# A convolution mixed by a softmax over kernel sets on one core: weights loaded by three transfers of 128 partitions instead of six of 64, and the first weight points computed ahead of the scale

## The chip, the cores and the metric

The kernel runs on one core of a Trainium2 chip. The metric is the device time of one execution in microseconds, as the median of the runs. Every duration below is from one profiled execution of the kernel before. Engines are called by the names of the profile: PE is TensorE (PEld its weight loads), DVE is VectorE, ACT is ScalarE, POOL is GpSimd, SP is SyncE, which only issues DMA transfers here.

## What is computed

The input is 8 images of 64 channels, 48 x 48 pixels. It is normalised over groups of two channels, then a 1x1 convolution with a bias and a softmax give 8 mixing weights for each pixel, and 8 different 3x3 convolutions (the "sets") of the normalised image are mixed with them. The input is added back.

```python
sel = softmax(conv1x1(gn(x), coupler_w) + coupler_b, axis=1)
sel = sel / sel.sum(axis=1, keepdims=True)
w = transpose(weight, (2, 0, 1, 3, 4)).reshape(s * oc, ic, k, k)     # 8 * 64 outputs
conv = conv3x3(gn(x), w, padding=1).reshape(b, s, oc, h, w) + bias[None, None, :, None, None]
out = x + einsum('bschw,bshw->bchw', conv, sel)
```

## The kernel before

**Tiling.** Two images make a round: 64 channels of each fill the 128 partitions, four rounds in all. Two pixels that are neighbours in a row are computed together: instead of three horizontal taps for each of them, four "points" of the input (sums and differences of columns, `v_pts`) are multiplied by four points of the weights (`w_pts`, and the raw first and third tap), which saves a third of the products. A tile is 128 pixel pairs; a round has 18 tiles. The products run in 16 bits: each operand is split into a head and a tail (what the head left out), so for each tile and point PE runs three matmuls of 128 x 512 with the heads (L375) and one or two with tails (L383, L387). The tails of two kernel rows are stacked on the two halves of the partitions, so the weights have to stand on partitions 0 to 63 and once more on 64 to 127.

**The rounds.** DVE turns the first two products into starting values in PSUM (`seed`, L690, L692), PE adds the last two points, DVE multiplies by the mixing weights (`multiply`, L706, L707) and adds halves (`halve`, L715), POOL adds the rest and the input (L1007 to L1017). Three sets of PSUM banks go round between PE and DVE.

**The preparation.** Before the first round the weights have to be made. All of it is an order written out by hand, one list for each engine:

- SP issues the three thirds of the first input `x_raw` (L306), two small matrices (L307), and then the weights `w_raw` (L310): for each half of the partitions (`w_low`, then `w_high`) three transfers, one for each kernel row r, of 64 partitions by 1536 floats. The weight tensor in memory has 64 rows, so each is read twice. After them SP waits for the first heads and copies them into the operand tile `op` (`first_fill`, L282 to L291).
- ACT adds up the absolute weights of each kernel row as it lands, as a bound for them (`bound_of`, L556 to L562, on the lower partitions; the accumulator is read out behind it). Between the first and second bound stands `first_heads(1, 0)` (L512), the first half of the input's point 1; behind the third `first_heads(0, 0)`.
- DVE takes statistics of the input, makes point 0 of the input in two parts (`first_input_point`, L877), tails (`input_tails_of`, L882), and for each kernel row a sum of the outer taps (`kernel_sum`, L835) and with it weight point 1 (`kernel_point1`, L840), later point 2 for all rows at once (`kernel_point2`, L846). `weight_bound` (L889) reduces the three bounds, PE spreads the result over the partitions (L444, L445; ahead of it in PE's queue stand 60 small matmuls of `warm_small`, L435), and `scales` (L894 to L901) makes the scale by which all heads of weights are cast.
- From the scale on, ACT casts weight heads (`w_heads_of`, L553), DVE makes tails of point 1 (`first_point_tails`, L821), which PE's first tile waits for (L383), and so on through the second and the last points to the first `seed`.

In `kernel_sum` DVE waits for both halves, one of which is the fourth transfer:

```python
dve.wait_ge(w_high[r], 16)
dve.wait_ge(w_low[r], 16)
```

Of the kernel before, what the change touches and what calls it, by code (L numbers as in the profile page):

```python
# [33 lines left out]
IMAGES, C, H, W = 8, 64, 48, 48  # L34
SETS, K = 8, 3
# [7 lines left out]
N = SETS * C  # L43
# [33 lines left out]
def program(nc, x, x_pix, weight, bias, coupler_w, coupler_b, matrices, out):  # L77
    with ExitStack() as ctx:
        def sb(name, shape, dt=F32):
            return ctx.enter_context(nc.sbuf_tensor(name, shape, dt))  # L80

        def sem(name):
            return ctx.enter_context(nc.semaphore(name))


        w_raw = sb("w_raw", [P, K, K, N])
# [71 lines left out]

        mats_loaded = sem("mats_loaded")
        small_loaded = sem("small_loaded")  # L160
        w_low = [sem(f"w_low{r}") for r in range(K)]
        w_high = [sem(f"w_high{r}") for r in range(K)]
        ready = sem("ready")
        cleared = sem("cleared")
        w_bounds = sem("w_bounds")
# [83 lines left out]
        def _(sp):  # L249
# [21 lines left out]
            def first_fill(g, part):  # L271

                pts = slice(2 * g, 2 * g + 2)
                heads_made, tails_made, landed, fifth = ((h_first, t_first, first_in[g], first_in[g]),
                                                         (h_done, t_done, ops_in[0][g], rest_in[g]))[part]
                cols = slice(0, PW + FIRST_PAIRS) if part == 0 else slice(PW + FIRST_PAIRS, PADDED)
                width = cols.stop - cols.start
                below = slice(0, FIRST_PAIRS) if part == 0 else slice(FIRST_PAIRS, PAIRS)
                above = slice(below.start + PW, below.stop + PW)
                heads = v_head[0:C, pts, :]  # L280
                wait(heads_made, 2 * g + 2)
                sp.dma_start(op[0][0:C, 0, pts, cols], heads[:, :, cols]).then_inc(landed, 16)  # L282
                sp.dma_start(op[0][0:C, 1, pts, cols], heads[:, :, cols]).then_inc(fifth, 16)
                sp.dma_start(op[0][C:P, 1, pts, below], heads[:, :, above]).then_inc(landed, 16)
                if g == 0:
                    sp.dma_start(op_two[0][C:P, :, cols], v_head[0:C, 1, cols].unsqueeze(1).to_broadcast([C, 2, width])) \
                        .then_inc(landed, 16)
                else:
                    sp.dma_start(op_two[0][0:C, :, cols], heads[:, :, cols]).then_inc(landed, 16)
                wait(tails_made, 2 * g + 2)  # L290
                sp.dma_start(op[0][C:P, 0, pts, cols], v_tail[0:C, pts, cols]).then_inc(landed, 16)  # L291
# [13 lines left out]
            for k in range(LOADS):  # L305
                sp.dma_start(*x_part(0, k)).then_inc(x_loaded[k], 16)  # L306
            sp.dma_start(mats[:, :, :], matrices).then_inc(mats_loaded, 16)  # L307
            for half_p, loaded in ((0, w_low), (1, w_high)):
                for r in range(K):
                    sp.dma_start(w_raw[C * half_p:C * half_p + C, r, :, :].rearrange("p b n -> p (b n)"),  # L310
                                 weight[:, r, :]).then_inc(loaded[r], 16)
            first_fill(0, 0)
            first_fill(1, 0)
            first_fill(0, 1)
# [154 lines left out]
        def _(act):  # L469
# [34 lines left out]
            def first_heads(k, part):  # L504

                act.wait_ge(scale_ready, 1)
                act.wait_ge(v_first[k], ((1, 2), (2, 3), (2, 3), (2, 3))[k][part])
                if k >= 2 and part == 0:
                    edge(0, k)
                    act.wait_ge(edge_done, k - 1)  # L510
                lo, hi = ((0, FIRST_PAIRS), (FIRST_PAIRS, PAIRS))[part]
                act.activation(v_head[:, k, PW + lo:PW + hi], v_pts[:, k, lo:hi], ACT.Copy, scale=norm_scale[:, 0:1]) \  # L512
                    .then_inc((h_first, h_done)[part], 1)
# [34 lines left out]
            def w_heads_of(k, rows=slice(0, K)):  # L548

                if k < 2:  # L550
                    act.wait_ge((w_point1, w_point2)[k], (rows.stop, 1)[k])
                src = w_pts[:, k, rows, :] if k < 2 else w_raw[:, rows, 2 * (k - 2), :]
                act.activation(w_head[:, k, rows, :], src, ACT.Copy,  # L553
                               scale=half_scale[:, 0:1] if k < 2 else scale[:, 0:1]).then_inc(w_heads[k], 1)

            def bound_of(r):  # L556

                act.wait_ge(w_low[r], 16)
                if r:
                    act.wait_ge(w_bounds, r)  # L560
                act.activation(w_pts[0:C, 1, :, :], w_raw[0:C, r, :, :], ACT.Abs, accum_out=w_max_part[0:C, r:r + 1]) \
                    .then_inc(w_bounds, 1)  # L562
# [9 lines left out]
            first_heads(1, 0)  # L572
            bound_of(1)
            bound_of(2)
            first_heads(0, 0)
            act.wait_ge(w_chain, W_STEPS)
            w_heads_of(0, slice(0, 1))
            first_heads(1, 1)
            first_heads(0, 1)
            w_heads_of(0, slice(1, 2))  # L580
            w_heads_of(0, slice(2, 3))
            first_heads(2, 0)
            w_heads_of(1)
            first_heads(3, 0)
            for r in range(K):
                act.wait_ge(w_high[r], 16)
            w_heads_of(2)
            copy_m1(0, 0)
            w_heads_of(3)
# [13 lines left out]
        def _(dve):  # L603
# [213 lines left out]
            def first_point_tails():  # L817

                for r, lo, hi, slot in ((0, 0, C, 0), (1, C, P, 0), (2, 0, P, 1)):
                    dve.wait_ge(w_heads[0], r + 1)  # L820
                    dve.scalar_tensor_tensor(w_tail[lo:hi, 0, slot, :], w_pts[lo:hi, 0, r, :], half_scale[lo:hi, 0:1],  # L821
                                             w_head[lo:hi, 0, r, :], ALU.mult, ALU.subtract).then_inc(w_tails, 1)
# [7 lines left out]

            def kernel_sum(r):

                dve.wait_ge(w_high[r], 16)
                dve.wait_ge(w_low[r], 16)
                dve.tensor_tensor(w_sum[:, r, :], w_raw[:, r, 0, :], w_raw[:, r, 2, :], ALU.add).then_inc(w_sums, 1)  # L835

            def kernel_point1(r):

                dve.wait_ge(w_sums, r + 1)
                dve.tensor_tensor(w_pts[:, 0, r, :], w_sum[:, r, :], w_raw[:, r, 1, :], ALU.add).then_inc(w_point1, 1)  # L840
# [18 lines left out]
            def coupler_parts():  # L859

                cw = cw_pair[:, :, :].rearrange("p b s -> p (b s)")
                cw_two = cw.unsqueeze(1).to_broadcast([P, 2, 2 * SETS])
                dve.wait_ge(w_chain, W_STEPS)
                dve.tensor_scalar(cw_pts[:, 0, 1:3, :], cw_two, half_scale[:, 1:2], None, ALU.mult)
                dve.tensor_scalar(cw_pts[:, 0, 0, :], cw, minus_half_scale[:, 1:2], None, ALU.mult).then_inc(c_heads, 1)
                dve.wait_ge(c_heads, 1)
                dve.scalar_tensor_tensor(cw_pts[:, 1, 1:3, :], cw_two, half_scale[:, 1:2], cw_pts[:, 0, 1:3, :],
                                         ALU.mult, ALU.subtract)
                dve.scalar_tensor_tensor(cw_pts[:, 1, 0, :], cw, minus_half_scale[:, 1:2], cw_pts[:, 0, 0, :],
                                         ALU.mult, ALU.subtract).then_inc(c_tails, 1)  # L870

            def first_input_point(part):
                rows = (slice(0, FIRST_ROWS), slice(FIRST_ROWS, H))[part]
                v_out, even, odd = point_operands(0, rows)
                dve.wait_ge(prep, 6)
                dve.wait_ge(scale_ready, 1)
                dve.scalar_tensor_tensor(v_out, even, twice_mean[:, 0:1], odd, ALU.subtract, ALU.add).then_inc(v_first[0], 1)  # L877

            def input_tails_of(k, part, nth):
                lo, hi = ((0, FIRST_PAIRS), (FIRST_PAIRS, PAIRS))[part]  # L880
                dve.wait_ge((h_first, h_done)[part], nth)
                dve.scalar_tensor_tensor(v_tail[:, k, PW + lo:PW + hi], v_pts[:, k, lo:hi], norm_scale[:, 0:1],  # L882
                                         v_head[:, k, PW + lo:PW + hi], ALU.mult, ALU.subtract) \
                    .then_inc((t_first, t_done)[part], 1)
# [30 lines left out]
            scale_and_shift(0)  # L915
            first_input_point(0)
            input_tails_of(1, 0, 1)
            first_input_point(1)
            kernel_sum(0)
            weight_bound()  # L920
            kernel_point1(0)
            scales()
            input_tails_of(0, 0, 2)
            kernel_sum(1)
            kernel_point1(1)
            coupler_parts()
            kernel_sum(2)
            kernel_point1(2)
            first_point_tails()
            kernel_point2()  # L930
            input_tails_of(1, 1, 1)
# [177 lines left out]
```

## Time and profile before

| what | us |
|---|---|
| median of 3 runs | 350.68 (350.5 to 350.99) |
| the profiled execution: its time | 350.75 |
| its span | 348.9 |
| PE busy | 326.7 (94%) |
| DVE busy | 286.2 (82%) |
| POOL busy | 229.4 (66%) |
| ACT busy | 93.8 (27%) |

PE is busy nine tenths and more of nearly all slices after the first seventh of the span. What PE loses, it loses ahead of that. The span stands 1.85 us below the execution's own time. A row of a timeline gives start and duration in us, the engine, line and operation, and in brackets how long the engine had been idle and what released it.

### The profile page before, as it was taken

What the parts mean: (1) busy time and instruction counts of PE and PEld (TensorE: products, weight loads), DVE (VectorE), ACT (ScalarE), POOL (GpSimd) and SP (SyncE); (2) the same over time, 40 slices, a digit from 0 to 9 for tenths busy, and PEclk for the clock granted to TensorE, in tenths of its full rate; (3) what the DMA queues carried; (4) which work ended last, traced back from release to release, by engine and by line L of the source; (5) the groups of instructions that cost most, each with busy time, mean ns of one, the idle gap of its engine ahead of it and who ended that gap; (6) DMA issues with size and microseconds to landing.
All of it is one profiled execution on the core that took longest, in us unless ns stands there. A gap on an engine that the chain in (4) does not pass through costs nothing.

```text
span 348.9 us, 5537 instructions
## 1 busy us (share of the span) xinstructions
PE 326.7 (94%) x1730; PEld 156.0 (45%) x1730; DVE 286.2 (82%) x503; ACT 93.8 (27%) x131; POOL 229.4 (66%) x329
## 2 busy tenths in 40 slices
PE   8858679989999999999999999999999999999993
PEld 8824234434444344444544344444544344444441
DVE  2599999978689879987699699987699697777776
ACT  1657401144611201145521111155411111111110
POOL 4420079999994467999964667999874489533343
PEclk9996899999999999999999999999999999999998
DMA  6952979902993099105891199007950397002002
GB/s 187 213 115 46 266 155 218 204 0 61 239 238 85 2 240 220 27 0 154 190 253 27 42 230 212 1 0 195 181 109 0 78 241 170 0 9 61 0 0 68
DMA packets 30274, 41.30 MB, mean 118 GB/s; under 512 B 2160, under 2 KB 23280, under 8 KB 29872
## 3 DMA queue, kind: packets, MB, share of 16 engines
q1 hardware_dynamic: 29376, 37.49, 47.0%
q10 hardware_dynamic: 880, 3.58, 3.5%
q8 instruction: 10, 0.16, 0.2%
q14 instruction: 8, 0.07, 0.1%
HBM read 11.97 MB, written 4.72 MB: 48 GB/s over the span
## 4 chain that ended last, share of the span: by engine, by line
PE 59%; DVE 20%; POOL 11%; issue 6%; DMA 2%; DVEq 1%; POOLq 0%; SPq 0%
PE pair L375 35%; PE pair L387 12%; PE pair L383 9%; DVE high L707 3%; DVE pair L706 3%; DMA x_raw<-x 2%; DVE pair L690 2%; POOL quarter L1007 2%; PE w_bank L435 2%; DVE pair L692 2%; POOL v_pts L981 2%; POOL x_res L1000 1%; POOL v_tail L973 1%; POOL bias_part L995 1%; DVE half L715 1%
## 5 line engine op out<-in xcount | busy, mean ns | idle before, releaser
L375 PE MATMUL pair<-w_head,op 128*128 128x512 f16 x864 | 235.9, 382 | 12.1 <-DMA op<-v_tail 5.3
L375 PEld LDWEIGHTS pair<-w_head,op 128*128 128x128 f16 x864 | 83.3, 98 | 117.5 <-DVE half L715 10.5
L387 PE MATMUL pair<-w_tail,op 128*128 128x512 f16 x288 | 110.3, 383 | 0.0
L532 ACT ACTIVATE m_sb<-pair 128x512 f32<-128x512 f32 x72 | 42.9, 596 | 224.6 <-PE pair L387 223.7
L1007 POOL TENSOR_TENSOR quarter<-half 128x256 f32<-128x256 f32 x71 | 52.7, 742 | 66.6 <-DVE half L715 66.4
L706 DVE TENSOR_TENSOR pair<-pair,sel_now 128x512 f32<-128x512 f32 x71 | 49.5, 697 | 36.9 <-PE pair L387 36.2
L715 DVE TENSOR_TENSOR half<-pair,high 128x512 f32<-128x512 f32 x71 | 49.1, 692 | 9.5
L383 PE MATMUL pair<-w_tail,op_two 128*128 128x512 f16 x144 | 55.1, 383 | 0.0
L690 DVE TENSOR_TENSOR pair<-pair,m_sb 128x512 f32<-128x512 f32 x72 | 49.6, 688 | 0.0
L692 DVE TENSOR_TENSOR pair<-m_sb,pair 128x512 f32<-128x512 f32 x72 | 49.3, 685 | 0.0
L707 DVE TENSOR_TENSOR high<-pair,sel_now 128x512 f32<-128x512 f32 x71 | 48.3, 681 | 0.0
L387 PEld LDWEIGHTS pair<-w_tail,op 128*128 128x128 f16 x288 | 28.2, 98 | 35.0 <-DVE w_tail L856 0.6
L1011 POOL TENSOR_TENSOR mixed<-quarter 128x128 f32<-128x128 f32 x71 | 33.0, 465 | 5.6
L1017 POOL TENSOR_TENSOR y_out<-mixed,x_res 128x128 f32<-128x128 f32 x71 | 32.2, 454 | 5.8 <-POOL mixed L1011 0.5
L973 POOL TENSOR_TENSOR v_tail<-v_pts,v_head 128x576 f16<-128x576 f32 x24 | 30.2, 1278 | 0.0
L383 PE MATMUL pair<-w_tail,op 128*128 128x512 f16 x72 | 27.8, 386 | 0.9 <-DVE w_tail L821 0.9
L1000 POOL TENSOR_TENSOR x_res<-x_res,bias_part 128x384 f32<-128x384 f32 x24 | 23.9, 997 | 2.3
L981 POOL TENSOR_TENSOR v_pts<-x_raw 128x1152 f32<-128x1152 f32 (+1 forms) x12 | 24.9, 2079 | 0.0
L383 PEld LDWEIGHTS pair<-w_tail,op_two 128*128 128x128 f16 x144 | 14.2, 98 | 17.2 <-issue 0.3
L995 POOL TENSOR_TENSOR bias_part<-bias_all,sel_now 128x384 f32<-128x384 f32 x24 | 19.9, 828 | 0.1
L606 DVE BATCH_NORM_STATS2 stats<-x_raw 128x6 f32<-128x384 f32 x24 | 11.9, 547 | 6.3 <-DMA x_raw<-x 6.3
L1063 POOL TENSOR_TENSOR v_pts<-v_pts,norm_scale 128x576 f32<-128x576 f32 x2 | 2.3, 1146 | 22.2 <-DVE sel_now L681 22.1
(96 smaller groups left out, 193.3 us busy)
## 6 DMA issues: line engine op xcount, KB each, us to landing
op<-v_head SPq DMA_DIRECT2D x14, 600.0 KB, 8.1
x_res<-x_pix SPq DMA_DIRECT2D x8, 576.0 KB, 6.6
op_two<-v_head SPq DMA_DIRECT2D x14, 300.0 KB, 9.2
op<-v_tail SPq DMA_DIRECT2D x14, 300.0 KB, 6.9
op<-v_head SPq DMA_DIRECT2D x14, 288.0 KB, 8.5
out<-y_out SPq DMA_DIRECT2D x7, 576.0 KB, 3.9
x_raw<-x ACTq DMA_DIRECT2D x3, 1152.0 KB, 10.6
w_raw<-weight SPq DMA_DIRECT2D x6, 384.0 KB, 11.5
```

What stands on the lines that cost most here:

```text
L375: nc.tensor.matmul(dst, op[b][:, 0, j, at + r * PW:at + r * PW + P], w_head[:, j, r, :], start=fresh and r == 0, stop=False, skip_group_ch ...
L383: nc.tensor.matmul(dst, op[b][:, 0, j, after] if j == 0 else op_two[b][:, j - 2, after], w_tail[:, j, 1, :], start=False, stop=False, skip ...
L387: return nc.tensor.matmul(dst, op[b][:, 1, j, at:at + P], w_tail[:, j, 0, :], start=False, stop=True, skip_group_check=True)
L532: act.activation(m1_sb[:, i % LOOK, :], pair[i % SETS_OF_BANKS][:, 0, :], ACT.Copy).then_inc(m1_copied, 1)
L690: dve.tensor_tensor(plus, minus, m1, ALU.add).then_inc(seeded, 1)
L692: dve.tensor_tensor(minus, m1, minus, ALU.subtract).then_inc(seeded, 1)
L706: dve.tensor_tensor(sets_of(i, 0), sets_of(i, 0), weights_of(i, 0), ALU.mult).then_inc(low_done, 1)
L707: dve.tensor_tensor(high[:, :, :, :], sets_of(i, SETS // 2), weights_of(i, SETS // 2), ALU.mult) \
L715: dve.tensor_tensor(half[:, i % LOOK, :, :, :].rearrange("p a s c -> p a (s c)"), pair[i % SETS_OF_BANKS][:, :, 0:N // 2], high[:, :, :, : ...
L973: last = pool.tensor_tensor(v_tail[:, k, PW + lo:PW + hi], v_pts[:, k, lo:hi], v_head[:, k, PW + lo:PW + hi], ALU.subtract)
L1007: pool.tensor_tensor(quarter[:, :, :, :].rearrange("p a s c -> p a (s c)"), hf[:, :, 0:2, :].rearrange("p a s c -> p a (s c)"), hf[:, :, 2 ...
L1011: pool.tensor_tensor(mixed[:, :, :], quarter[:, :, 0, :], quarter[:, :, 1, :], ALU.add).then_inc(mixed_done, 1)
```

## The change

The host lays the 64 rows of the weights out twice, one below the other, so that one transfer of 128 partitions brings a kernel row to both halves: three transfers take the place of six, with one semaphore each (`w_loaded[r]`). The bytes that are moved are the same. On DVE the sums and first weight points of rows 0 and 1 stand ahead of `weight_bound`, with `first_input_point(1)` between them, and `coupler_parts` stands behind those of row 2. On ACT the three casts of weight point 1 follow each other, ahead of two input heads.

```diff
-            for half_p, loaded in ((0, w_low), (1, w_high)):
-                for r in range(K):
-                    sp.dma_start(w_raw[C * half_p:C * half_p + C, r, :, :].rearrange("p b n -> p (b n)"),
-                                 weight[:, r, :]).then_inc(loaded[r], 16)
+            for r in range(K):
+                sp.dma_start(w_raw[:, r, :, :].rearrange("p b n -> p (b n)"), weight[:, r, :]).then_inc(w_loaded[r], 16)
...
             def bound_of(r):
 
-                act.wait_ge(w_low[r], 16)
+                act.wait_ge(w_loaded[r], 16)
...
             w_heads_of(0, slice(0, 1))
+            w_heads_of(0, slice(1, 2))
+            w_heads_of(0, slice(2, 3))
             first_heads(1, 1)
             first_heads(0, 1)
-            w_heads_of(0, slice(1, 2))
-            w_heads_of(0, slice(2, 3))
             first_heads(2, 0)
             w_heads_of(1)
             first_heads(3, 0)
-            for r in range(K):
-                act.wait_ge(w_high[r], 16)
             w_heads_of(2)
...
             def kernel_sum(r):
 
-                dve.wait_ge(w_high[r], 16)
-                dve.wait_ge(w_low[r], 16)
+                dve.wait_ge(w_loaded[r], 16)
...
             input_tails_of(1, 0, 1)
+            kernel_sum(0)
+            kernel_point1(0)
             first_input_point(1)
-            kernel_sum(0)
+            kernel_sum(1)
+            kernel_point1(1)
             weight_bound()
-            kernel_point1(0)
             scales()
             input_tails_of(0, 0, 2)
-            kernel_sum(1)
-            kernel_point1(1)
-            coupler_parts()
             kernel_sum(2)
             kernel_point1(2)
+            coupler_parts()
             first_point_tails()
...
-    weight = np.asarray(L0_conv_weight).transpose(1, 3, 4, 2, 0).reshape(C, K, K * N)
+    weight = np.tile(np.asarray(L0_conv_weight).transpose(1, 3, 4, 2, 0).reshape(C, K, K * N), (2, 1, 1))
```

DVE's list before, from the first tails of the input to the input's tails behind the scale (`w_sum` is `kernel_sum`, `w_pts<-w_sum` is `kernel_point1`, `w_max` is `weight_bound`, L894 to L901 are `scales`):

```order
14 L882 SCALAR_TENSOR_TENSOR v_tail<-v_pts,norm_scale,v_head 128x576
15 L877 SCALAR_TENSOR_TENSOR v_pts<-x_raw,twice_mean 128x576
16 L835 TENSOR_TENSOR w_sum<-w_raw 128x512
17 L889 TENSOR_REDUCE w_max<-w_max_part 64x1
18 L840 TENSOR_TENSOR w_pts<-w_sum,w_raw 128x512
19 L894 TENSOR_SCALAR magnitude<-w_bank 128x2
...
25 L882 SCALAR_TENSOR_TENSOR v_tail<-v_pts,norm_scale,v_head 128x576
26 L835 TENSOR_TENSOR w_sum<-w_raw 128x512
27 L840 TENSOR_TENSOR w_pts<-w_sum,w_raw 128x512
28 L864 TENSOR_SCALAR cw_pts<-cw_pair,half_scale 128x32
```

The same place in the changed kernel (its lines are numbered six lower here):

```order
14 L876 SCALAR_TENSOR_TENSOR v_tail<-v_pts,norm_scale,v_head 128x576
15 L829 TENSOR_TENSOR w_sum<-w_raw 128x512
16 L834 TENSOR_TENSOR w_pts<-w_sum,w_raw 128x512
17 L871 SCALAR_TENSOR_TENSOR v_pts<-x_raw,twice_mean 128x576
18 L829 TENSOR_TENSOR w_sum<-w_raw 128x512
19 L834 TENSOR_TENSOR w_pts<-w_sum,w_raw 128x512
20 L883 TENSOR_REDUCE w_max<-w_max_part 64x1
21 L888 TENSOR_SCALAR magnitude<-w_bank 128x2
...
27 L876 SCALAR_TENSOR_TENSOR v_tail<-v_pts,norm_scale,v_head 128x576
28 L829 TENSOR_TENSOR w_sum<-w_raw 128x512
29 L834 TENSOR_TENSOR w_pts<-w_sum,w_raw 128x512
30 L858 TENSOR_SCALAR cw_pts<-cw_pair,half_scale 128x32
```

Ahead of `w_max` DVE now has two pairs of sum and point instead of one sum; between `w_max` and the scale's first step nothing is left; behind the scale there is one pair where there were two (the second of them stood behind the four `cw_pts` rows).

ACT's list before, from the scale on (L553 casts weight heads, L512 input heads):

```order
10 L553 ACTIVATE w_head<-w_pts,half_scale 128x512
11 L512 ACTIVATE v_head<-v_pts,norm_scale 128x576 x2
12 L553 ACTIVATE w_head<-w_pts,half_scale 128x512 x2
13 L475 ACTIVATE v_pts<-x_raw,group 128x48
14 L512 ACTIVATE v_head<-v_pts,norm_scale 128x576
```

And in the changed kernel:

```order
10 L550 ACTIVATE w_head<-w_pts,half_scale 128x512 x3
11 L509 ACTIVATE v_head<-v_pts,norm_scale 128x576 x2
12 L472 ACTIVATE v_pts<-x_raw,group 128x48
13 L509 ACTIVATE v_head<-v_pts,norm_scale 128x576
```

The two input heads now stand behind the third weight cast, which waits for the weight point of kernel row 2.

## Rows read from the trace of the kernel before

**Rows 1.** The page, busy time: engine, us, share of span, instructions.
```profile
PE 326.7 (94%) x1730; PEld 156.0 (45%) x1730; DVE 286.2 (82%) x503; ACT 93.8 (27%) x131; POOL 229.4 (66%) x329
```

**Rows 2.** Busy time in stretches, with the names of its columns.
```profile
core 0: us, PE busy (x) PEld busy (x) DVE busy (x) ACT busy (x) POOL busy (x), PEclk, DMA share, GB/s
38.55:41.95 3.40, 3.40 (x10) 1.01 (x7) 3.31 (x7) 0.60 (x1) 0.00 (x0) 0.51 0.94 324
41.95:47.40 5.45, 2.59 (x11) 0.90 (x10) 5.00 (x11) 0.00 (x0) 2.22 (x2) 0.99 1.14 246
47.40:349.00 301.60, 292.29 (x1495) 133.41 (x1495) 250.78 (x432) 72.30 (x102) 217.68 (x303) 0.99 0.47 110
```

**Rows 3.** Waits from 47 us on: who for whom, total us, times, longest.
```profile
DVE pair L706 <- PE pair L387: 36.2, 36, 2.9
PE pair L375 <- DVE half L715: 5.1, 5, 2.5
```

**Rows 4.** Timeline of DVE from the first input point to the bound.
```profile
13.12 0.82 DVE L877 SCALAR_TENSOR_TENSOR v_pts<-x_raw,twice_mean 128x576 f32<-128x576 f32 x1
14.39 0.82 DVE L882 SCALAR_TENSOR_TENSOR v_tail<-v_pts,norm_scale,v_head 128x576 f16<-128x576 f32 x1 [0.46 <-ACT v_head L512]
15.12 0.81 DVE L877 SCALAR_TENSOR_TENSOR v_pts<-x_raw,twice_mean 128x576 f32<-128x576 f32 x1
17.60 0.69 DVE L835 TENSOR_TENSOR w_sum<-w_raw 128x512 f32<-128x512 f32 x1 [1.67 <-DMA w_raw<-weight]
18.21 0.14 DVE L889 TENSOR_REDUCE w_max<-w_max_part 64x1 f32<-64x3 f32 x1
```

**Rows 5.** Timeline of ACT, the bounds and the first input head.
```profile
12.11 1.49 ACT L561 ACTIVATE w_pts<-w_raw 64x1536 f32<-64x1536 f32 x1 [7.21 <-DMA w_raw<-weight]
...
13.60 0.76 ACT L512 ACTIVATE v_head<-v_pts,norm_scale 128x576 f16<-128x576 f32 x1
...
15.91 1.49 ACT L561 ACTIVATE w_pts<-w_raw 64x1536 f32<-64x1536 f32 x1
```

**Rows 6.** Single issues: third input part, first and last weight transfer, and landing.
```profile
L306 SPq DMA_DIRECT2D x_raw<-x x1: 424/424/424, 1.7 to 1.7; - x1
DMA to landing us min/median/max: 7.7/7.7/7.7
...
L310 SPq DMA_DIRECT2D w_raw<-weight x1: 1452/1452/1452, 2.6 to 2.6; - x1
DMA to landing us min/median/max: 9.5/9.5/9.5
...
L310 SPq DMA_DIRECT2D w_raw<-weight x1: 610/610/610, 6.8 to 6.8; - x1
DMA to landing us min/median/max: 14.8/14.8/14.8
```

**Rows 7.** Stretches again: first the input loads, then weights alone.
```profile
6.00:7.00 1.00, 1.00 (x11) 1.00 (x11) 0.77 (x2) 0.00 (x0) 0.72 (x1) 1.00 1.06 396
...
12.00:18.00 6.00, 6.00 (x56) 6.00 (x55) 3.14 (x7) 5.80 (x8) 0.55 (x1) 1.00 1.00 210
```

**Rows 8.** Timeline of DVE behind the scale.
```profile
19.73 0.81 DVE L882 SCALAR_TENSOR_TENSOR v_tail<-v_pts,norm_scale,v_head 128x576 f16<-128x576 f32 x1
...
21.17 1.19 DVE L840 TENSOR_TENSOR w_pts<-w_sum,w_raw 128x512 f32<-128x512 f32 x1
...
23.55 0.69 DVE L835 TENSOR_TENSOR w_sum<-w_raw 128x512 f32<-128x512 f32 x1
...
24.88 2.31 DVE L821 SCALAR_TENSOR_TENSOR w_tail<-w_pts,half_scale,w_head 64x512 f16<-64x512 f32 x3
```

**Rows 9.** Timeline of PE: warm-up, first product, first product with a tail.
```profile
11.45 6.95 PE L435 MATMUL w_bank<-ones 128*128 128x128 f32 x60
...
24.63 0.74 PE L375 MATMUL pair<-w_head,op 128*128 128x512 f16 x2 [2.89 <-DMA op<-v_tail]
...
27.24 0.61 PE L383 MATMUL pair<-w_tail,op 128*128 128x512 f16 x1 [0.86 <-DVE w_tail L821]
```

More of the change, by code:

```diff
@@ L160, in program @@
         small_loaded = sem("small_loaded")
-        w_low = [sem(f"w_low{r}") for r in range(K)]
-        w_high = [sem(f"w_high{r}") for r in range(K)]
+        w_loaded = [sem(f"w_loaded{r}") for r in range(K)]
         ready = sem("ready")
```

## The prediction

> **What bounds the kernel now.** I read the busy times first. PE is busy for 326.7 us of a span of 348.9, DVE for 286.2 [rows 1]. The stretches show that these two do not bound the same part: from 47.4 us on PE works 292.3 of 301.6 us at the full granted clock, while from 41.95 to 47.4 it works 2.6 of 5.45 us and DVE 5.0 [rows 2]. The waits behind 47 us say the same: DVE waits 36.2 us for PE there, PE only 5.1 us for DVE [rows 3]. So the rounds are a block of PE work, of which the change touches nothing, and what can be won is the moment at which the block begins. That moment is the end of a preparation which DVE carries. The timeline of DVE shows only two waits of size in it behind 13 us: 0.46 us for ACT, and 1.67 us for a weight transfer, up to 17.60 [rows 4]. From there it works almost without a gap to 47. Whatever moves this chain moves the end by as much; the median (350.68) and the profiled execution (350.75) differ by 0.07 us, which I neglect.
>
> **The transfers.** The first weight transfer is issued at 2.6 us and lands 9.5 us later, at 12.1; the last, issued at 6.8, lands 14.8 us later, at 21.6 [rows 6]. Five transfers of 384 KB in 9.5 us are 1.9 us each, about 207 GB/s, and the stretch in which only weights flow has 210 GB/s with the DMA engines 1.00 busy. One stretch of 1 us, in which it is mostly the input (128 partitions) that flows, has 396 GB/s at the same full share [rows 7]. The engines are full in both, so a packet of the weights takes twice its time, and what differs is that the weights go to 64 partitions. With 128 partitions I take 396 GB/s: a transfer of 768 KB (786,432 bytes) takes 2.0 us. The third input part lands at 1.7 + 7.7 = 9.4 us [rows 6]; the first weight transfer lands 2.7 us behind it, 1.9 for its bytes and 0.8 for its way. I keep 0.2 to 0.8 of the latter: the kernel rows land at about 11.9, 13.9 and 15.9 us, earliest 11.6, 13.6, 15.6. By the other end, the rate of today, they need the time of two old transfers each: 14.0, 17.8 and 21.6. I choose the fast end, since the row with 128 partitions is the one that resembles the new transfer.
>
> The page "SBUF — State Buffer" of the Trainium skill (Door 1) says that a range of 64 partitions reaches only 8 of the 16 ports that transfers use, so by it the rate doubles; it would give the fast landings. The page "DMA: Bandwidth & Descriptors" (Rules for kernel authors) says of two transfers to disjoint halves that they share the same 16 engines and follow each other, and advises one transfer; read by its reason alone, the engines, nothing would be gained, which is the slow end.
>
> SP issues three transfers in place of six; it next waits for a head that ACT makes only behind its third bound, so the issue time of 0.6 us each [rows 6] costs and gives nothing.
>
> **ACT up to the scale.** The first bound starts at 11.9 instead of 12.11 and takes 1.49; the input head behind it starts about 13.4 to 13.6 and takes 0.76 [rows 5]. The third bound today starts 2.3 us behind that head and would start then at 15.9 with the row just landed; it ends about 1.6 us later, at 17.5 (its accumulator is read out behind it), as now.
>
> **DVE up to the scale.** DVE's first input point starts at 13.12 and the tails start between 14.0 and 14.39, when the head is ready [rows 4, 5]. Behind the tails (0.73 from start to start) come pair 0, the second input point (0.8) and pair 1, where a pair is a sum and a weight point. A pair takes 24.88 - 23.55 = 1.33 us where nothing disturbs it [rows 8]. From 14.2 this ends at 14.2 + 0.73 + 1.33 + 0.8 + 1.33 = 18.4 us; the bound is reduced there, against 18.21 before [rows 4]. The idle 1.67 us and the point that lay in the wait for PE have been filled with work. PE could not have answered sooner than 18.40, when its 60 small matmuls end (11.45 + 6.95, [rows 9]). So the scale comes at the same time or 0.2 us later; I put 0.1. While PE answers, DVE now idles; that is the cover which pair 0's point gives up.
>
> **DVE behind the scale.** Input tails at 19.73, then two pairs and the four small coupler steps, then the weight tails at 24.88 [rows 8]. The change leaves one pair. The point at 21.17 takes 1.19 instead of 0.69, beside work of POOL that the first weight cast releases; that slot stays, filled by the pair of kernel row 2. What goes is a pair of 1.33 us. The coupler steps stay on the path. Sum: -1.33 + 0.1 = -1.2 us; the weight tails start at 23.7.
>
> **What waits for it.** PE's first products start at 24.63, released by the operand transfers, and its first product with a tail at 27.24, released by DVE's tail [rows 9]. With tails 1.2 us earlier PE goes on at 26.0, so the operand copies have 1.4 us of slack even if they do not move. On ACT the third weight cast stands ahead of two input heads and waits for the point of kernel row 2, which ends at 21.2 + 0.1 + 1.2 = 22.5 us [rows 8]: one cast and two heads of 0.76 each [rows 5] end at 24.8. DVE asks for them only behind its weight tails and the point 2 that follows, after 26 us, so this move costs nothing; if the point came 1.5 us later it would begin to. ACT's three waits for the upper halves fall out; they are over before it reaches them, so they give nothing. From point 2 on every engine follows DVE, which has no gap in which 1.2 us could get lost, up to the first `halve`, which releases the PE block at 47.4.
>
> **Forecast**: 350.75 - 1.2 = 349.5 us. If the inputs land a little sooner too, since the slow weight packets of other engines no longer lie beside the last of them, there is up to 0.7 us more; that PE's warm-up stands in line behind the statistics lets it come through. I put 0.1 of it: 349.4. Its own range is 348.7 to 350.0.
>
> **Rivals.**
> 1. The transfers gain less. The third bound must end by 18.3, so kernel row 2 must land by 16.7. The three transfers after 9.4 + 0.5 then have 6.8 us for 2.36 MB, or 347 GB/s. For: 396 GB/s is one stretch of 1 us. At 300 GB/s the row lands at 17.8, 1.1 us late, and the gain is 0.1 us: 350.6. Chance 0.13.
> 2. The transfers gain nothing, because the engines and not the partitions set the pace. Then kernel row 2 lands at 21.6, its bound ends at 23.2, the bound is reduced at 23.3 against 18.21, 5.1 us later, and DVE, which has its pairs 0 and 1 behind it, starts its weight tails 5.1 - 1.33 = 3.8 us later: 354.5 us. It is slower from a landing of about 17.9 on. Against: full share at 396 as well as at 210 GB/s [rows 7]. Chance 0.09.
> 3. The clock. From 38.55 to 41.95 PE was granted half [rows 2], behind an idle stretch, while DVE bounded. PE idles again for 2.5 us ahead of 47.4 [rows 3], without a fall. If the shifted work meets the clock otherwise and such a stretch of 3.4 us falls behind the start of the PE block, it costs half of it, 1.7 us: 351.1. Chance 0.07.
>
> The forecast has 0.68, and 0.03 are left for a gain beyond 348.7. The range of 8 in 10 runs from 348.7 to 351.2: it leaves out rival 2 and what is below. A measurement of this kernel can tell about 0.2% (0.7 us) from no change. Faster by more than that is the forecast's case and the gain beyond it: 0.71, with part of rival 1 0.73. Within 0.2% are the rest of rival 1 and rival 3: 0.17. Slower is rival 2 and its neighbours: 0.10.
>
> **What would show it.** The three weight transfers should land by 12, 14 and 16 us, the stretch from 10 to 15 us should have near 390 GB/s, and DMA should be nearly idle at 17. DVE should have no wait for weights; `magnitude` should start at 19.1 to 19.3, the weight tails at 23.7, PE's first product with a tail at 26.0, and the first `halve` should end near 46.2. A landing of kernel row 2 behind 17 us makes the forecast wrong, and so does a stretch at half clock behind 46 us.

## The result, and the profile after

The changed kernel takes 348.88 us (median of 5 runs, 348.82 to 349.19), against 350.68 before (350.5 to 350.99). The ratio is 0.9948, with a 95% interval of 0.9937 to 0.9959: 1.8 us or 0.5% faster. Forecast were 349.4 us in a range of 348.7 to 351.2; the result lies inside it, but only 0.2 us above its lower end. The span of the profiled execution fell from 348.9 to 346.8, by 2.1 us, where the sum of the prediction had 1.2, or 1.3 with its allowance. The time of that execution fell by less, from 350.75 to 348.88: 0.2 us were lost outside the span, and no row shows where.

The rows of the page on busy time, to be read against [rows 1], show that no work was saved: DVE, ACT and POOL are busy as long as before. PE is busy for 1.9 us more with the same 1730 matmuls. It was granted half its clock for longer, ahead of the block of the rounds (the third number from the end is the granted clock), where DVE sets the pace:

```profile
span 346.8 us, 5530 instructions
...
PE 328.6 (95%) x1730; PEld 157.4 (45%) x1730; DVE 286.2 (83%) x503; ACT 93.8 (27%) x131; POOL 229.4 (66%) x329
...
37.60:44.00 6.40, 5.45 (x13) 1.52 (x12) 6.02 (x13) 0.00 (x0) 0.99 (x1) 0.50 1.07 271
```

In the kernel before that stretch was 3.4 us long, at 0.51 [rows 2].

The single issues of the changed kernel, the third input part and the first and last weight transfer, with their way to landing, answer to [rows 6]:

```profile
L305 SPq DMA_DIRECT2D x_raw<-x x1: 424/424/424, 1.7 to 1.7; - x1
DMA to landing us min/median/max: 6.7/6.7/6.7
...
L308 SPq DMA_DIRECT2D w_raw<-weight x1: 1345/1345/1345, 2.6 to 2.6; - x1
DMA to landing us min/median/max: 8.0/8.0/8.0
...
L308 SPq DMA_DIRECT2D w_raw<-weight x1: 712/712/712, 4.7 to 4.7; - x1
DMA to landing us min/median/max: 9.7/9.7/9.7
```

The input is complete at 1.7 + 6.7 = 8.4 us instead of 9.4; kernel row 0 at 2.6 + 8.0 = 10.6, kernel row 2 at 4.7 + 9.7 = 14.4. The last weights of the kernel before landed at 21.6. Between the two weight rows lie 3.8 us for two transfers of 768 KB, 1.9 us each or 414 GB/s. Busy time in stretches of the changed kernel says the same in its last two columns, the share of the DMA engines and GB/s (to be read against [rows 7]):

```profile
9.00:12.00 3.00, 3.00 (x29) 3.00 (x28) 1.29 (x7) 1.34 (x1) 3.00 (x5) 1.00 1.01 424
...
15.00:18.00 3.00, 2.93 (x27) 2.77 (x26) 2.54 (x5) 2.08 (x3) 0.00 (x0) 1.00 0.00 0
```

The timeline of DVE in the changed kernel, from the scale of the input to the weight tails, is the chain of [rows 4] and [rows 8]:

```profile
12.31 0.15 DVE L623 TENSOR_SCALAR norm_scale<-rstd 128x1 f32<-128x1 f32 x1 [0.81 <-POOL rstd L956]
12.58 0.82 DVE L871 SCALAR_TENSOR_TENSOR v_pts<-x_raw,twice_mean 128x576 f32<-128x576 f32 x1
13.32 0.81 DVE L876 SCALAR_TENSOR_TENSOR v_tail<-v_pts,norm_scale,v_head 128x576 f16<-128x576 f32 x1
14.05 0.69 DVE L829 TENSOR_TENSOR w_sum<-w_raw 128x512 f32<-128x512 f32 x1
...
17.44 0.14 DVE L883 TENSOR_REDUCE w_max<-w_max_part 64x1 f32<-64x3 f32 x1
18.34 0.16 DVE L888 TENSOR_SCALAR magnitude<-w_bank 128x2 int32<-128x2 int32 x1 [0.76 <-PE w_bank L442]
...
18.95 0.81 DVE L876 SCALAR_TENSOR_TENSOR v_tail<-v_pts,norm_scale,v_head 128x576 f16<-128x576 f32 x1
19.68 0.68 DVE L829 TENSOR_TENSOR w_sum<-w_raw 128x512 f32<-128x512 f32 x1
20.40 1.19 DVE L834 TENSOR_TENSOR w_pts<-w_sum,w_raw 128x512 f32<-128x512 f32 x1
...
22.77 2.31 DVE L816 SCALAR_TENSOR_TENSOR w_tail<-w_pts,half_scale,w_head 64x512 f16<-64x512 f32 x3
```

Both waits of [rows 4] are gone; DVE waits for PE instead, for 0.76 us, ahead of the scale. The bound is reduced at 17.44 instead of 18.21, and the weight tails start at 22.77 instead of 24.88, 2.11 us earlier. That is what arrives at the end of the span. On PE the same two rows as in [rows 9] (timeline of PE, changed kernel):

```profile
22.87 0.82 PE L372 MATMUL pair<-w_head,op 128*128 128x512 f16 x3 [1.91 <-DMA op<-v_tail]
...
25.13 0.61 PE L380 MATMUL pair<-w_tail,op 128*128 128x512 f16 x1 [1.44 <-DVE w_tail L816]
```

The operands come 1.8 us earlier too, and PE still waits for DVE's tail (1.44 us).

### The profile page after: what moved, and what is told of

It is laid out like the page before. It is cut to its first block, busy times and chain, and to the rows that moved or that the text cites. A ratio compares the mean times of both kernels' runs of the same rounds, so it can differ in the third digit from the quotient of the medians.

```text
span 346.8 us, 5530 instructions
## 1 busy us (share of the span) xinstructions
PE 328.6 (95%) x1730; PEld 157.4 (45%) x1730; DVE 286.2 (83%) x503; ACT 93.8 (27%) x131; POOL 229.4 (66%) x329
## 4 chain that ended last, share of the span: by engine, by line
PE 62%; DVE 20%; POOL 11%; issue 6%; DVEq 1%; POOLq 0%
PE pair L372 35%; PE pair L384 12%; PE pair L380 9%; PE w_bank L432 5%; DVE high L702 3%; DVE pair L701 3%; DVE pair L685 2%; POOL quarter L1001 2%; DVE pair L687 2%; POOL v_pts L975 2%; POOL x_res L994 1%; POOL v_tail L967 1%; DVE half L710 1%; POOL bias_part L989 1%; POOL mixed L1005 1%
## 5 line engine op out<-in xcount | busy, mean ns | idle before, releaser
L380 PEld LDWEIGHTS pair<-w_tail,op_two 128*128 128x128 f16 x144 | 14.2, 99 | 18.0 <-DVE w_tail L847 0.8
L432 PE MATMUL w_bank<-ones 128*128 128x128 f32 x116 | 15.9, 306 | 1.5 <-POOL v_tail L1032 1.5
L432 PEld LDWEIGHTS w_bank<-ones 128*128 128x128 f32 x116 | 15.6, 221 | 1.5 <-POOL v_tail L1032 1.5
```

Of the source, the lines that this page charges most:

```text
L380: nc.tensor.matmul(dst, op[b][:, 0, j, after] if j == 0 else op_two[b][:, j - 2, after], w_tail[:, j, 1, :], start=False, stop=False, skip ...
L432: nc.tensor.matmul(w_bank[:, 2 * P:3 * P], ones[:, :], ones[:, :], start=True, stop=True)
```

## Experiments

Each kernel ran beside the kernel before on the same chip; its ratio is to that kernel there. "Tails at" is the start of the three weight tails (`first_point_tails`) on DVE in the profiled execution.

| kernel | tails at, us | span, us | difference | median, us | ratio, 95% interval |
|---|---|---|---|---|---|
| before | 24.88 | 348.9 | 324.0 | 350.68 | 1 |
| changed | 22.77 | 346.8 | 324.0 | 348.88 | 0.9948 [0.9937, 0.9959] |
| transfers_only | 23.52 | 347.6 | 324.1 | 349.80 | 0.9971 [0.9950, 0.9992] |
| order_only | 26.76 | 350.9 | 324.1 | 352.27 | 1.0036 [1.0016, 1.0056] |
| act_old | 22.80 | 346.9 | 324.1 | 348.89 | 0.9944 [0.9923, 0.9966] |
| six_full | 22.75 | 347.4 | 324.7 | 349.26 | 0.9957 [0.9936, 0.9979] |
| middle | 29.01 | 353.0 | 324.0 | 355.07 (one run) | |
| x_first | 25.59 | 349.6 | 324.0 | 351.46 (one run) | |
| warm26 | 22.88 | 347.0 | 324.1 | 349.07 | 0.9950 [0.9935, 0.9964] |
| cover | 22.74 | 346.8 | 324.1 | 348.32 | 0.9923 [0.9895, 0.9952] |
| cover_warm26 | 22.13 | 346.2 | 324.1 | 348.24 | 0.9923 [0.9909, 0.9937] |
| pool_early | 21.84 | 345.9 | 324.1 | 348.02 | 0.9923 [0.9893, 0.9953] |

In eleven of the twelve rows the span ends 324.0 to 324.1 us behind the start of the weight tails, though that start moves over 7 us. That is the shift one for one which the prediction assumed. (The medians come from four batches; the kernel before had 350.68 in the first, then 350.77 beside the four rows from `transfers_only` to `six_full`, 350.95 beside `middle`, `x_first`, `warm26` and `cover_warm26`, and 350.73 beside `cover` and `pool_early`.)

### transfers_only: new transfers, old orders

```diff
-            kernel_sum(0)
-            kernel_point1(0)
             first_input_point(1)
-            kernel_sum(1)
-            kernel_point1(1)
+            kernel_sum(0)
             weight_bound()
+            kernel_point1(0)
             scales()
             input_tails_of(0, 0, 2)
-            kernel_sum(2)
-            kernel_point1(2)
+            kernel_sum(1)
+            kernel_point1(1)
             coupler_parts()
+            kernel_sum(2)
+            kernel_point1(2)
```

with ACT's list of the kernel before as well.

> Theory (the gain of about 2.1 us is two terms that add: scale 0.78 us earlier, since the input and the weights land earlier, and one pair of sum and point, 1.33 us, gone from behind the scale): with the old orders and the new transfers the scale comes as early as in the changed kernel (DVE's magnitude at 18.3 us), but two pairs stand behind it, so the weight tails start at 24.1 and the time is 0.8 us below before, near 349.9. Rival A (the landings are all, DVE catches up by itself): weight tails at 22.8 and 348.9. Rival B (the landings alone give nothing, since DVE's order held it): 350.7.

Measured: 349.80 us, and tails at 23.52. Neither start that the expectation gave for the tails (24.1, 22.8) was met, nor the scale at 18.3, though the time lay near the theory's 349.9. Timelines of DVE and then of PE in this kernel:

```profile
14.76 0.68 DVE L829 TENSOR_TENSOR w_sum<-w_raw 128x512 f32<-128x512 f32 x1
16.43 0.15 DVE L883 TENSOR_REDUCE w_max<-w_max_part 64x1 f32<-64x3 f32 x1 [0.98 <-ACT w_pts L558]
...
17.77 0.16 DVE L888 TENSOR_SCALAR magnitude<-w_bank 128x2 int32<-128x2 int32 x1 [0.60 <-PE w_bank L442]
...
10.45 6.95 PE L432 MATMUL w_bank<-ones 128*128 128x128 f32 x60
17.23 0.28 PE L441 MATMUL w_bank<-tiny,ones 128*128 128x2 f32 x2
```

With one sum instead of two pairs ahead of it the bound is reduced as soon as ACT has it, at 16.43, and the scale's first step comes at 17.77, not at 18.34 as in the changed kernel. The bound is 1.0 us earlier and the scale only 0.57, because PE takes up its part only at 17.23, when its 60 small matmuls are through: here the warm-up holds the scale, not the bound. So the landings alone move the tails by 24.88 - 23.52 = 1.36 us. The new order makes the scale 0.57 us later again and takes 1.33 us from behind it: 0.76 by the two rows, 0.75 measured (23.52 - 22.77). The two parts of the change are worth 1.36 and 0.75 us in the profiled executions; in the medians 0.97 and, across two batches, about 0.9.

### order_only: old transfers, new orders

DVE's and ACT's lists of the changed kernel on the six transfers of 64 partitions.

> Theory: with the old six transfers the sum of kernel row 0 waits at the head of DVE's list for the fourth transfer (17.6 us), that of row 1 for the fifth (19.4), so the bound is reduced near 21.1 instead of 18.2; with one pair less behind it the weight tails start 2.9 - 1.33 = 1.6 us later than before, at 26.5, and the time is near 352.3. Rival (the order is worth its 1.33 us by itself): 349.4.

Measured: 352.27 us, tails at 26.76, 1.9 us later than before; the theory held, with the bound at 21.02 where 21.1 had been put. Of the two waits that it named only the first occurred, 2.40 us for the fourth transfer; the fifth had landed (6.2 + 13.3 = 19.5 us) when DVE came to it at 19.70. Timelines of DVE and then of PE:

```profile
17.63 0.69 DVE L835 TENSOR_TENSOR w_sum<-w_raw 128x512 f32<-128x512 f32 x1 [2.40 <-DMA w_raw<-weight]
...
18.97 0.81 DVE L877 SCALAR_TENSOR_TENSOR v_pts<-x_raw,twice_mean 128x576 f32<-128x576 f32 x1
19.70 0.68 DVE L835 TENSOR_TENSOR w_sum<-w_raw 128x512 f32<-128x512 f32 x1
...
21.02 0.14 DVE L889 TENSOR_REDUCE w_max<-w_max_part 64x1 f32<-64x3 f32 x1
...
21.31 0.56 PE L444 MATMUL w_bank<-tiny,ones 128*128 128x2 f32 x2 [2.98 <-DVE w_max L889]
```

The second input point, which needs no weights at all, stands behind a sum that waits for them. The tails came 0.26 us later than forecast, mostly since PE was slower with its part of the scale: it had been idle for 2.98 us behind its small matmuls, the granted clock was 0.50 from 21.3 to 22.3 us, and its two steps took 0.56 and 0.57 us instead of 0.35 and 0.36 in the changed kernel. The order by itself makes the kernel slower, and is worth something only on top of the transfers.

### act_old: the changed kernel with ACT's old list

```diff
             w_heads_of(0, slice(0, 1))
-            w_heads_of(0, slice(1, 2))
-            w_heads_of(0, slice(2, 3))
             first_heads(1, 1)
             first_heads(0, 1)
+            w_heads_of(0, slice(1, 2))
+            w_heads_of(0, slice(2, 3))
```

> The changed kernel with ACT's old order of casts and input heads. Theory: the move on ACT costs and gives nothing, since DVE asks for these products only behind its weight tails: within 0.2 us of the changed kernel, 348.9. Rival (the third weight cast is needed sooner, and two heads ahead of it hold up the tails): the third weight tail waits, 0.3 to 0.7 us slower, 349.2 to 349.6.

Measured: 348.89 us and tails at 22.80, no difference. The move on ACT is worth nothing, as forecast.

### six_full: is it the number of transfers?

```diff
             for r in range(K):
-                sp.dma_start(w_raw[:, r, :, :].rearrange("p b n -> p (b n)"), weight[:, r, :]).then_inc(w_loaded[r], 16)
+                for c in range(2):
+                    half_n = slice(c * (K * N // 2), (c + 1) * (K * N // 2))
+                    sp.dma_start(w_raw[:, r, :, :].rearrange("p b n -> p (b n)")[:, half_n], weight[:, r, half_n]) \
+                        .then_inc(w_loaded[r], 16)
...
-                act.wait_ge(w_loaded[r], 16)
+                act.wait_ge(w_loaded[r], 32)
```

with the same 32 in `kernel_sum`.

> The changed kernel, but each transfer of 128 partitions x 6 KB is cut into two of 128 partitions x 3 KB, so there are six transfers of 384 KB as before the change. Theory (64 partitions halve the rate): packets of 3 KB at the input's rate, the last weights land by 14.4 to 15 us, time as the changed kernel, 348.9 plus at most 0.2. Rival (fewer and larger transfers are what made it fast): landings every 1.9 us for each 384 KB, the last near 20 us or later, and a time above 351.

Measured: the sixth transfer of this kernel (single issue, from the trace) lands at 6.4 + 8.1 = 14.5 us, as the third did in the changed kernel.

```profile
L310 SPq DMA_DIRECT2D w_raw<-weight x1: 437/437/437, 6.4 to 6.4; - x1
DMA to landing us min/median/max: 8.1/8.1/8.1
```

The number and size of the transfers have no part in it. The tails start at 22.75 as well. The time was 349.26 us, 0.4 above the changed kernel instead of at most 0.2, and this is the one row of the table whose difference is longer (324.7); the intervals of the two ratios overlap. The 0.6 us of that execution lie in the rounds. Timelines of POOL, first in the changed kernel, then in `six_full`:

```profile
49.02 0.99 POOL L994 TENSOR_TENSOR x_res<-x_res,bias_part 128x384 f32<-128x384 f32 x1
...
49.55 1.00 POOL L997 TENSOR_TENSOR x_res<-x_res,bias_part 128x384 f32<-128x384 f32 x1 [0.62 <-DMA x_res<-x_pix]
```

POOL waits 0.62 us for the pixels that are added back (`x_res`), and stays 0.55 us behind up to its first step of the next normalisation, at 70.42 us instead of 69.87, for which DVE and then PE wait. In the changed kernel the same transfer lands at 36.5 + 12.1 = 48.6 us, just ahead of its use at 49.02. So the rule of one for one has little room left there: a kernel whose rounds start earlier can be held by this transfer, and the second profile of `cover_warm26` (below) waits 0.23 us for it. Whether the other executions of the changed kernels near 350 us have this cause is not shown.

### middle: 64 partitions, but others

```diff
-            for r in range(K):
-                sp.dma_start(w_raw[:, r, :, :].rearrange("p b n -> p (b n)"), weight[:, r, :]).then_inc(w_loaded[r], 16)
+            for lo, hi in ((32, 96), (0, 32), (96, 128)):
+                for r in range(K):
+                    sp.dma_start(w_raw[lo:hi, r, :, :].rearrange("p b n -> p (b n)"), weight[lo:hi, r, :]) \
+                        .then_inc(w_loaded[r], 16)
```

and the waits for a kernel row ask for all three of its transfers.

> The changed kernel, but the weights come as three transfers to partitions 32 to 95, then three to 0 to 31, then three to 96 to 127; the orders wait for all. Theory A (what halves the rate is that 0 to 63 and 64 to 127 each reach only half of the ports, by partition number): 64 partitions that straddle the middle run at full rate, their 384 KB land about 1.0 us apart, and the outer 32 at half rate. Theory B (64 partitions as a number halve the rate): the first three land 1.9 us apart, as before the change. The time is above the changed kernel in both, by the late landing of the outer parts.

Measured: 355.07 us. Busy time in stretches of this kernel, first where only the 64 middle partitions are being filled (the input is complete at 8.4 us), then the outer ones:

```profile
8.50:10.00 1.50, 1.50 (x15) 1.33 (x13) 1.24 (x4) 0.00 (x0) 1.50 (x3) 1.00 1.01 418
...
11.00:12.00 1.00, 1.00 (x11) 1.00 (x11) 0.19 (x2) 0.00 (x0) 1.00 (x2) 1.00 0.97 197
12.00:15.00 3.00, 3.00 (x29) 3.00 (x29) 0.97 (x2) 0.00 (x0) 0.28 (x1) 1.00 1.02 219
```

64 partitions that straddle the middle run at 418 GB/s, 0 to 31 and 96 to 127 at about 200. So it is not the count of partitions but which ones. Nor is it the tensor laid out twice in memory, from which both kinds are read. The landings did not follow the forecast: they came 1.7 to 1.8 us apart (9.7, 11.4 and 13.2 us), not 1.0, which taken alone is nearer to the 1.9 of theory B; it is the rate of the stretch, 1.5 us of one execution, that decides. A likely reason is that the engines were not level, so that the fastest were with the outer partitions while the last still had middle ones to write; no view shows the single engines. The page "SBUF — State Buffer" of the Trainium skill (Door 1) gives the rule by partition number: 0 to 63 reach the same 8 ports as 0 to 31, and the next 64 the other 8. The 418 GB/s of partitions 32 to 95, which by it reach all 16, agree. The page "DMA: Bandwidth & Descriptors" of the Trainium skill (Rules for kernel authors) says that transfers to the two halves follow each other, because they share the same engines either way. They did, and its advice, one transfer of 128 partitions, is right; but shared engines alone do not give the gain. The engines were full in both cases (1.00 and 1.01), and 1.9 us brought 384 KB before and 768 KB after.

### x_first: the input's gain

```diff
+            wait(x_loaded[LOADS - 1], 16)
             for half_p, loaded in ((0, w_low), (1, w_high)):
```

This is the kernel before, with its weight transfers held back until the input has landed.

> The kernel before, with a wait of SP for the third input part ahead of the weight transfers. Theory (in the kernel before, weight packets to 64 partitions held up the last input packets): the third input part lands at 8.4 us instead of 9.4, as in the changed kernel, and DVE's norm_scale comes at 12.3 instead of 12.84. Rival (the earlier landing in the changed kernel has another cause, such as fewer issues): it lands at 9.4 as before. The time is worse than before by the later weights, above 353, in both.

Measured: the third input part lands at 1.7 + 6.6 = 8.3 us, as in the changed kernel, and `norm_scale` comes at 12.37 instead of 12.84. The theory on the cause holds: in the kernel before weight packets of the slow kind lay beside the last input packets. Single issue of x_first:

```profile
L306 SPq DMA_DIRECT2D x_raw<-x x1: 426/426/426, 1.7 to 1.7; - x1
DMA to landing us min/median/max: 6.6/6.6/6.6
```

The forecast of a time above 353 was wrong (351.46, one run): the weights are issued 5.7 us later, but the first lands at 8.3 + 4.5 = 12.8 us, 0.7 behind before. An early issue buys little where the queue ahead is full.

### cover, warm26 and both: what holds the scale now

In the changed kernel DVE is idle for 0.76 us while PE answers. `cover` moves one point into that gap:

```diff
             kernel_sum(1)
-            kernel_point1(1)
             weight_bound()
+            kernel_point1(1)
             scales()
```

`warm26` takes 4 of the 30 small matmuls (8 of 60 in the trace, 0.9 us) out of PE's queue ahead of its part, which are there only to keep it busy (`order_only` shows its part behind an idle stretch); `cover_warm26` does both.

> The changed kernel with the point of kernel row 1 moved behind the reduction of the bound, and the warm-up as it was. Theory (the reduction at 17.44 us and the end of PE's warm-up at 17.4 to 17.7 stand side by side, so neither alone is worth much): the bound is reduced at 16.8, PE answers only from 17.4 to 17.7 on, so 0.1 to 0.4 us is gained: 348.6 to 348.8. Rival (DVE's idle wait alone holds the scale): 0.65 us gained, 348.2.

> The changed kernel with 26 instead of 30 small matmuls ahead of PE's part of the scale. Theory: the warm-up ends at 16.7 instead of 17.66, but DVE reduces the bound only at 17.44 to 17.58, so at most 0.1 us is gained: 348.8. Rival (the warm-up alone holds the scale): 0.7 us gained, 348.2.

> The changed kernel with the point of kernel row 1 moved behind the reduction of the bound (into DVE's idle 0.76 us while PE answers) and 26 instead of 30 small matmuls ahead of PE's part (0.93 us less). Theory: the bound is reduced at 16.8, PE is free at 16.7, the scale comes 0.65 us sooner and everything behind it too: 348.2. Rival (PE's clock falls earlier and stays at half into the rounds): 349 or more.

> The kernel with both, again: 348.2, ratio 0.9925, and below the changed kernel on the same chip by 0.6 to 0.7 us.

> The changed kernel once more, on the chip of the three that follow: 348.9, ratio 0.995.

Measured on one chip: changed kernel 348.99 (0.9947, interval 0.9929 to 0.9965), `cover` 348.32, `cover_warm26` 348.27 (0.9921, interval 0.9893 to 0.9950). In the batch before it `cover_warm26` had 348.24 and `warm26` 349.07. The warm-up alone is worth nothing, both together 0.7 us, and `cover` alone nearly as much: the 0.65 us of its rival, against its theory's 0.1 to 0.4. Its profiled execution is not typical: it is the slowest of its seven runs, 348.85 us. Timelines of PE, first in `cover`, then in `cover_warm26`:

```profile
10.99 6.94 PE L432 MATMUL w_bank<-ones 128*128 128x128 f32 x60
17.77 0.28 PE L441 MATMUL w_bank<-tiny,ones 128*128 128x2 f32 x2
```

```profile
10.50 6.05 PE L432 MATMUL w_bank<-ones 128*128 128x128 f32 x52
17.09 0.35 PE L441 MATMUL w_bank<-tiny,ones 128*128 128x2 f32 x2 [0.54 <-DVE w_max L883]
```

In `cover` PE's warm-up began at 10.99 and held its part until 17.77, with the bound ready at 17.0. Among the eleven traces of kernels with the new transfers (`middle` among them) it begins between 10.40 and 10.56 in eight, and at 10.71, 10.74 and 10.99 in three. With a start at 10.45 `transfers_only` took up the same part at 17.23 and had the scale's first step at 17.77, 0.54 us before the 18.31 of the trace of `cover`. An estimate from these rows is 348.85 - 0.54 = 348.31 us for an execution of `cover` with the usual start, and its median is 348.32. So the theory was wrong in its size: it let PE answer from 17.4 to 17.7 on, the end of the warm-up's row, and PE begins its part about 0.2 us ahead of that end. With 26 small matmuls PE waits 0.54 us for DVE and the scale no longer depends on the warm-up's start. The medians of the two do not differ by more than they scatter. All 12 executions of `cover_warm26` lie between 348.12 and 348.40 us, but `pool_early`, which has the same warm-up, has two of seven near 348.9, so that the shorter warm-up does away with the longer executions is not shown.

### pool_early: POOL beside DVE

```diff
             inverse_deviation(0)
-            pool.wait_ge(w_heads[0], 1)
             for k in range(2, NP):
                 raw_point(k, LOADS - 1)
```

on top of `cover_warm26`.

> As the kernel with both, but POOL makes its last two raw points at once instead of behind the first weight cast. They then run beside DVE's input point, tails and first pair (12.9 to 15.2 us) and not beside the pair and coupler steps behind the scale. Theory (what POOL slows is DVE's sum or point with two inputs, from 0.69 to 1.19 us, and the coupler step, not the input points and tails, at 0.81): of the 1.0 us that they cost behind the scale some 0.5 to 1.0 is gained, 347.3 to 347.7. Rival (any DVE step beside POOL's is slowed as much): no gain, 348.2 or slower.

Measured: 348.02 us, tails at 21.84 against 22.13. The timeline of DVE in this kernel:

```profile
12.61 1.10 DVE L871 SCALAR_TENSOR_TENSOR v_pts<-x_raw,twice_mean 128x576 f32<-128x576 f32 x1
13.62 1.36 DVE L876 SCALAR_TENSOR_TENSOR v_tail<-v_pts,norm_scale,v_head 128x576 f16<-128x576 f32 x1
...
20.51 0.69 DVE L834 TENSOR_TENSOR w_pts<-w_sum,w_raw 128x512 f32<-128x512 f32 x1
21.12 0.23 DVE L858 TENSOR_SCALAR cw_pts<-cw_pair,half_scale 128x32 f16<-128x32 f32 x1
```

Behind the scale the slowing is gone (0.69 instead of 1.19, 0.23 instead of 0.77: 1.04 us), but the input point and the tails take 1.10 and 1.36 instead of 0.82 and 0.81, 0.83 us more. The rival was nearer: DVE loses about as much wherever POOL's two points lie; 0.2 to 0.3 us remain. It is the fastest kernel seen by its median, 0.97 us below the changed kernel on the same chip (348.99), though its interval does not part it from `cover_warm26` and two of its seven runs took 348.85 and 348.95.

## Why the prediction was right, point by point

**The block behind the preparation** was right: the moment at which the weight tails start carries over one for one, in kernels from 21.84 to 29.01 us. The one exception is an execution of `six_full`, where a transfer that POOL waits for came late in the first round; the prediction did not look at that transfer.

**The rate of the transfers** was right, and chosen from the right row: 396 GB/s taken from one stretch of 1 us, 414 to 424 measured. The rows landed at 10.6 and 14.4 us, forecast 11.9 and 15.9: the size of the step (2.0 us) was nearly right, 1.9, but the place from which it was counted was the old landing of the input.

**The input** is the term that was mis-sized. "Up to 0.7 us more" was seen as possible, and 0.1 was put. The input landed 1.0 us earlier, and the input's tails on DVE start at 13.32, forecast 14.2. Of these 0.88 us, 0.53 are the earlier `norm_scale` (12.31 instead of 12.84); the rest came because the first bound on ACT, with kernel row 0 at 10.6, no longer stands in the way of the head. Behind them all steps took what they were given: 4.12 us to the bound (17.44 - 13.32), forecast 4.2. The scale came 0.78 us earlier where 0.1 later had been put, so 1.33 + 0.78 = 2.11 us instead of 1.2. `x_first` shows the cause of the first share (0.47 at `norm_scale` without the slow packets beside the input); the second is read from the two traces alone. The row for it was there: in the stretch from 6 to 7 us the input runs at 396 GB/s [rows 7], yet its last part needs until 9.4. From 7.4 to 10 us the kernel before moved 195 GB/s and the changed kernel 420. That the time still fell inside the range is owed in part to its width: the forecast gain of 1.3 us was 1.8, and the lower end allowed 2.0.

**The pair** of 1.33 us behind the scale was right to the row. The split that I gave to the two halves of the change after the result (0.8 for the landings, 1.33 for the order) was wrong: `transfers_only` gives 1.36 and 0.75, because the new order also delays the reduction of the bound. The split of 1.36 and 0.75 holds for this warm-up, which takes part of the gain of `transfers_only` away.

**The moves without a price** (ACT's casts, SP's issues, the operand copies) were right; `act_old` shows the first. (The 0.6 us for each issue is the last one of [rows 6]; the first took 1.45.)

**The rivals.** The first and second fell with the rate. The third, the clock, did occur, and its price was wrong. In the profiled execution of `transfers_only` PE was at half its clock (0.51, or 1.2 of 2.4 GHz) in a stretch just behind the start of the block (busy time in stretches, granted clock third from the end):

```profile
46.10:46.90 0.80, 0.80 (x4) 0.40 (x5) 0.80 (x2) 0.00 (x0) 0.66 (x2) 1.00 1.12 196
46.90:50.30 3.40, 3.40 (x10) 1.22 (x8) 3.27 (x7) 0.60 (x1) 3.24 (x4) 0.51 0.37 74
```

PE started 10 matmul records there instead of 16 in the 3.4 us behind 47.4 of the kernel before, but the span still ends 324.1 us behind the tails. DVE was busy for 3.27 of the 3.40 us: at the head of the rounds it is still DVE that sets the pace, so the 1.7 us of the rival were not lost. The prediction took the price of half the stretch from PE alone.

## What to carry to other kernels

A transfer's rate is to be looked up by the partitions that it reaches, not by its bytes or the share of the engines: the same bytes took half the time once both halves of the partitions were filled by one transfer, and the engines were "full" in both. Slow transfers are paid for by their neighbours too; here about a quarter of the gain (0.5 of 2.1 us, at `norm_scale`) came from an input that had been issued ahead of them. And an order that starts work earlier is worth its while only if the data are there: ahead of them it holds up what needs none.

## What the runs showed of the hardware

Partitions 32 to 95 were filled at 418 GB/s, 0 to 31 and 96 to 127 and, before the change, 0 to 63 and then 64 to 127, at 197 to 219 GB/s, all with the DMA engines about 1.0 busy. DVE's steps beside POOL's took 0.28 to 0.55 us longer, and a small step of 0.23 us took 0.77. PE's first 28 small matmuls of the kernel (56 in the trace) ended at times that differ between executions, from 9.4 us in the second trace of the changed kernel to 10.8 in that of `cover`; where they ended late they moved the warm-up's start, which lay between 10.40 and 10.99 us. In one execution 3.4 us at half the clock at the head of the rounds cost nothing, because DVE was busy for 3.27 of them.
